# Low value weights in 64 rows: two gates' low products in the two row halves of the array

## The reference, cut to what matters

```python
Pn = rmsnorm(P, input_norm_w)
k_proj, v_proj = Pn @ Wk.T, Pn @ Wv.T
for _ in range(3):
    q_proj = rmsnorm(slots, slot_norm_w) @ Wq.T
    attn = softmax(einsum('bkd,bmd->bkm', q_proj, k_proj) * SCALE, axis=-2)
    attn = attn / (sum(attn, axis=-1) + EPS)
    updates = einsum('bkm,bmd->bkd', attn, v_proj)
    gx, gh = updates @ wih.T + bih, slots @ whh.T + bhh
    r, z = sigmoid(xr + hr), sigmoid(xz + hz)
    n = tanh(xn + r * hn)
    slots = (1.0 - z) * n + z * slots
```

## Time and profile before

| | us |
|---|---|
| median of 3 runs | 1113.85 (1113.64 to 1114.71) |
| the profiled execution | 1113.94 |
| its span in the profile | 1112.2 |
| TensorE busy in the span | 1081.4 (97%) |
| VectorE busy | 779.3 (70%) |
| ScalarE busy | 547.1 (49%) |
| POOL busy | 340.8 (31%) |

### The profile page before, as it was taken

The page is one execution under the profiler, slowest core; times in us unless marked ns, Lnnn a source line. Parts: engine busy times, 40 slices in busy tenths (PEclk is TensorE's granted clock), DMA queues, the critical chain, the costliest instruction groups (busy, mean ns, idle before and its releaser), DMA issues.

```text
span 1112.2 us, 17705 instructions
## 1 busy us (share of the span) xinstructions
PE 1081.4 (97%) x6087; PEld 932.4 (84%) x6087; DVE 779.3 (70%) x1504; ACT 547.1 (49%) x830; POOL 340.8 (31%) x352
## 2 busy tenths in 40 slices
PE   6799999999999999999999999999999999999996
PEld 4588888888887878888888888888889888888896
DVE  7887687868689878888466666566665666656663
ACT  5365555555457843333455544544544554545442
POOL 6124444444206100000214242342333433324332
PEclk9899999999999999999999999999999999999998
DMA  7600110101226541222664543534435444344421
GB/s 246 151 1 16 23 34 6 28 11 24 91 73 193 152 125 23 27 30 27 169 210 103 142 97 132 152 90 137 112 121 148 99 128 135 102 144 116 117 34 20
DMA packets 61323, 105.39 MB, mean 95 GB/s; under 512 B 12128, under 2 KB 50272, under 8 KB 56928
## 3 DMA queue, kind: packets, MB, share of 16 engines
q1 hardware_dynamic: 44064, 83.05, 23.5%
q0 software_dynamic: 16512, 21.50, 12.0%
q10 hardware_dynamic: 704, 0.29, 0.1%
HBM read 74.11 MB, written 21.27 MB: 86 GB/s over the span
## 4 chain that ended last, share of the span: by engine, by line
PE 90%; DVE 6%; ACT 1%; issue 1%; DMA 1%; SPq 0%; POOL 0%; DVEq 0%; ACTq 0%
PE wide L1289 30%; PE down L1303 15%; PE wide L854 15%; PE wide L1142 8%; PE down L1154 4%; PE down L915 3%; PE wide L861 3%; PE wide L863 2%; PE wide L1335 2%; PE side L1275 1%; PE side L1126 1%; PE side L304 1%; PE down L1349 1%; PE side L939 1%; DVE pre L1706 1%
## 5 line engine op out<-in xcount | busy, mean ns | idle before, releaser
L2277 DVE SCALAR_TENSOR_TENSOR hid<-wide,b_up,silu 128x512 f32<-128x512 f32 x120 | 90.1, 751 | 161.5 <-PE wide L1289 152.9
L1289 PE MATMUL wide<-xt_hi,w_hi 128*128 128x512 f32 x480 | 188.6, 393 | 0.0
L1289 PE MATMUL wide<-xt_lo,w_hi 128*128 128x512 f32 x480 | 187.7, 391 | 0.0
L1289 PE MATMUL wide<-xt_hi,w_lo 128*128 128x512 f32 x480 | 186.9, 389 | 0.0
L825 POOL DMA_INDIRECT out_tokens<-y,idx_out x64 | 111.6, 1744 | 222.0 <-DVE y L2258 175.7
L1662 ACT ACTIVATE silu<-wide,b_gate 128x512 f32<-128x512 f32 x120 | 82.1, 684 | 143.7 <-PE wide L1289 143.7
L1303 PE MATMUL down<-w_hi,hid_hi 128*128 128x256 f32 x480 | 136.5, 284 | 0.0
L1303 PE MATMUL down<-w_lo,hid_hi 128*128 128x256 f32 x480 | 135.7, 283 | 0.0
L1303 PE MATMUL down<-w_hi,hid_lo 128*128 128x256 f32 x480 | 135.7, 283 | 0.0
L1671 ACT ACTIVATE hid_hi<-hid 128x512 fp32r<-128x512 f32 x120 | 76.0, 633 | 100.6 <-DVE hid L2277 100.6
L2228 DVE TENSOR_TENSOR w_lo<-raw,w_hi 128x768 fp32r<-128x768 f32 x128 | 121.5, 949 | 2.5 <-ACT w_hi L1636 2.5
(11 more groups left out here) (329 smaller groups left out, 2269.1 us busy)
## 6 DMA issues: line engine op xcount, KB each, us to landing
raw<-in_w_expert SPq DMA_DIRECT2D x32, 1536.0 KB, 6.3
x_raw<-in_x SPq DMA_DIRECT2D x16, 256.0 KB, 6.8
out_tokens<-slots SPq DMA_DIRECT2D x16, 256.0 KB, 3.7
token_rows<-work SPq DMA_DIRECT2D x8, 512.0 KB, 3.0
out_tokens<-y POOLq DMA_DIRECT2D x8, 512.0 KB, 5.9
attn<-rms_c SPq DMA_DIRECT2D x24, 128.0 KB, 2.3
attn<-expo SPq DMA_DIRECT2D x24, 128.0 KB, 2.3
x_first<-in_x SPq DMA_DIRECT2D x8, 256.0 KB, 3.1
```

What stands on the lines that cost most here:

```text
L1289: last = nc.tensor.matmul(bank[:, f % 2, :], w[f // HALF_F][:, f % HALF_F, (c + k) * P:(c + k + 1) * P], x_[:, k, :], start=(m == 1), stop ...
L2277: nc.vector.scalar_tensor_tensor(hid[:, f % 2, :], eup[:, f % 2, :], b_up[:, bass.ds(e, 1), f:f + 1].rearrange("p a b -> p (a b)"), silu[: ...
```

## The change

The tile vw_lo loses one of its two copies: for batch b of a pair, the columns of gates r and x lie in b's own 64 rows and those of gate z in the other 64 rows. The low attention no longer meets the low value weights: vw_lo is multiplied with the high attention alone, in 64 rows. For z that needs the high attention in the other rows too, so each half's high attention is also sent to a new tile attn_x (one for each pair), two more DMAs a half. TensorE closes r and z by `low_gates`: r's low product in b's rows and z's in the other rows, next to each other, behind z's high product. m_r is told there instead of right behind r's products. x's low product (`new_value`) has 64 rows and no partner. POOL subtracts in two instructions, z's 256 columns into vw_f, which SP then moves to the other rows by two DMAs a pair, and r's and x's 512 straight into vw_lo. To make room, the tile dif goes, and the mix works in place in slots.

```diff
-        vw_lo = att("vw_lo", [P, PAIRS, 2, 3 * D], F32R)
+        attn_x0 = att("attn_x0", [P, 2 * GROUP], F32R)
+        att.at += 2 * D * 4
+        vw_lo = att("vw_lo", [P, PAIRS, 3 * D], F32R)
...
-        dif = loop("dif", [P, KC, GROUP])
+        attn_x1 = loop("attn_x1", [P, 2 * GROUP], F32R)
+        attn_x = (attn_x0, attn_x1)
...
-            DMA_ATTN = 2 * 2 * 16
+            DMA_ATTN = 3 * 2 * 16
+            VW_MOVES = (4 + 2) * PAIRS
...
-                    sp.wait_ge(p_own, pair + 1)
-                    move_rows(vw_lo, vw_f, pair)
+                    sp.wait_ge(p_own, 2 * pair + 2)
+                    for b in range(2):
+                        sp.dma_start(vw_lo[rows_of(1 - b), pair, D:2 * D].bitcast(F32), vw_f[rows_of(b), pair, D:2 * D])\
+                            .then_inc(d_vw, 16)
...
                         sp.dma_start(attn[rows_of(b), pair, b, half].bitcast(F32), rms_c[rows_of(b), h, :]).then_inc(d_attn[h], 16)
+                        sp.dma_start(attn_x[pair][rows_of(1 - b), half].bitcast(F32), rms_c[rows_of(b), h, :])\
+                            .then_inc(d_attn[h], 16)
...
-                    nc.gpsimd.tensor_tensor(vw_f[:, pair, :].bitcast(F32R), vw_f[:, pair, :],
-                                            vw_own[:, pair, :].bitcast(F32), ALU.subtract).then_inc(p_own, 1)
+                    nc.gpsimd.tensor_tensor(vw_f[:, pair, D:2 * D].bitcast(F32R), vw_f[:, pair, D:2 * D],
+                                            vw_own[:, pair, D:2 * D].bitcast(F32), ALU.subtract).then_inc(p_own, 1)
+                    nc.gpsimd.tensor_tensor(gates_rx(vw_lo, pair), gates_rx(vw_f, pair), gates_rx(vw_own, pair).bitcast(F32),
+                                            ALU.subtract).then_inc(p_own, 1)
...
-                        nc.tensor.matmul(out[:, :], vw_hi[:, pair, b, cols], attn[:, pair, b, half],
-                                         start=start, stop=False)
-                        return nc.tensor.matmul(out[:, :], vw_lo[:, pair, b, cols], attn[:, pair, b, half],
-                                                start=False, stop=True)
+                        return nc.tensor.matmul(out[:, :], vw_hi[:, pair, b, f * P:(f + 1) * P], attn[:, pair, b, half],
+                                                start=start, stop=False)
+
+                    def low_gates():
+
+                        own, other = rows_of(b), rows_of(1 - b)
+                        nc.tensor.matmul(gate_r[:, :], vw_lo[own, pair, c * P:(c + 1) * P], attn[own, pair, b, half],
+                                         start=False, stop=True).then_inc(m_r, 1)
+                        nc.tensor.matmul(gate_z[:, :], vw_lo[other, pair, (2 + c) * P:(3 + c) * P], attn_x[pair][other, half],
+                                         start=False, stop=True).then_inc(m_z, 1)
+
+                    def new_value():
+
+                        own = rows_of(b)
+                        from_attention(gate_x, 4 + c, True)
+                        nc.tensor.matmul(gate_x[:, :], vw_lo[own, pair, (4 + c) * P:(5 + c) * P], attn[own, pair, b, half],
+                                         start=False, stop=True).then_inc(m_x, 1)
...
                         wait_attention()
-                        from_attention(gate_r, c, False).then_inc(m_r, 1)
-                        from_attention(gate_z, 2 + c, False).then_inc(m_z, 1)
+                        from_attention(gate_r, c, False)
+                        from_attention(gate_z, 2 + c, False)
+                        low_gates()
                     else:
                         if c == 0:
                             wait_attention()
-                        from_attention(gate_r, c, False).then_inc(m_r, 1)
+                        from_attention(gate_r, c, False)
                         if early is not None:
                             early()
                         pe.wait_ge(a_z, u + 1)
                         from_slots(gate_z, 2 + c, False)
-                        from_attention(gate_z, 2 + c, False).then_inc(m_z, 1)
+                        from_attention(gate_z, 2 + c, False)
+                        low_gates()
                         if between is not None:
                             between()
                         pe.wait_ge(a_h, u + 1)
                         from_slots(gate_h, 4 + c, True).then_inc(m_h, 1)
                     pe.wait_ge(v_pre, u + 1)
-                    from_attention(gate_x, 4 + c, True).then_inc(m_x, 1)
+                    new_value()
...
-                    nc.vector.tensor_tensor(dif[:, :, :], slots[:, :, sl], nn[:, :, :], ALU.subtract).then_inc(v_mix, 1)
+                    nc.vector.tensor_tensor(slots[:, :, sl], slots[:, :, sl], nn[:, :, :], ALU.subtract).then_inc(v_mix, 1)
```

More of the change, by code:

```diff
@@ L700, in _, with gates_rx @@
                                         ALU.subtract).then_inc(p_wlo, 1)
+                def gates_rx(tile, pair):
+                    return tile[:, pair, :].rearrange("p (a c) -> p a c", c=D)[:, 0:3:2, :]
                 for pair in range(PAIRS):
                     pool.wait_ge(a_own, pair + 1)
-                    nc.gpsimd.tensor_tensor(vw_f[:, pair, :].bitcast(F32R), vw_f[:, pair, :],
-                                            vw_own[:, pair, :].bitcast(F32), ALU.subtract).then_inc(p_own, 1)
+                    nc.gpsimd.tensor_tensor(vw_f[:, pair, D:2 * D].bitcast(F32R), vw_f[:, pair, D:2 * D],
+                                            vw_own[:, pair, D:2 * D].bitcast(F32), ALU.subtract).then_inc(p_own, 1)
+                    nc.gpsimd.tensor_tensor(gates_rx(vw_lo, pair), gates_rx(vw_f, pair), gates_rx(vw_own, pair).bitcast(F32),
+                                            ALU.subtract).then_inc(p_own, 1)
                 def low_of(g, run):
@@ L858, in from_attention @@
                     def from_attention(out, f, start):
-                        cols = slice(f * P, (f + 1) * P)
-                        nc.tensor.matmul(out[:, :], vw_hi[:, pair, b, cols], attn[:, pair, b, half],
-                                         start=start, stop=False)
-                        return nc.tensor.matmul(out[:, :], vw_lo[:, pair, b, cols], attn[:, pair, b, half],
-                                                start=False, stop=True)
+                        return nc.tensor.matmul(out[:, :], vw_hi[:, pair, b, f * P:(f + 1) * P], attn[:, pair, b, half],
[11 more added lines that the diff above has]
+                                         start=False, stop=True).then_inc(m_x, 1)
                     def wait_attention():
                         if u == 0:
-                            pe.wait_ge(d_vw, PAIRS * 8 * 16)
+                            pe.wait_ge(d_vw, VW_MOVES * 16)
+                            pe.wait_ge(p_own, 2 * PAIRS)
                         pe.wait_ge(d_attn[g4 % 2], DMA_ATTN * (2 * it + pair + 1))
@@ L1713, in gru_group @@
                     dve.wait_ge(a_n, u + 1)
-                    nc.vector.tensor_tensor(dif[:, :, :], slots[:, :, sl], nn[:, :, :], ALU.subtract).then_inc(v_mix, 1)
+                    nc.vector.tensor_tensor(slots[:, :, sl], slots[:, :, sl], nn[:, :, :], ALU.subtract).then_inc(v_mix, 1)
                     dve.wait_ge(v_mix, 2 * g + 1)
                     dve.wait_ge(a_z, u + 2)
-                    nc.vector.scalar_tensor_tensor(dif[:, :, :], tz[:, g4 % 2, :, :], 1.0, dif[:, :, :], ALU.add,
+                    nc.vector.scalar_tensor_tensor(slots[:, :, sl], tz[:, g4 % 2, :, :], 1.0, slots[:, :, sl], ALU.add,
                                                    ALU.mult).then_inc(v_mix, 1)
                     dve.wait_ge(v_mix, 2 * g + 2)
-                    nc.vector.scalar_tensor_tensor(slots[:, :, sl], dif[:, :, :], 0.5, nn[:, :, :], ALU.mult,
+                    nc.vector.scalar_tensor_tensor(slots[:, :, sl], slots[:, :, sl], 0.5, nn[:, :, :], ALU.mult,
                                                    ALU.add).then_inc(v_new, 1)
@@ L2033, in mix_half @@
                     dve.wait_ge(a_n, u + 1)
-                    nc.vector.tensor_tensor(dif[:, c, :], slots[:, c, sl], nn[:, c, :], ALU.subtract).then_inc(v_mix, 1)
+                    nc.vector.tensor_tensor(slots[:, c, sl], slots[:, c, sl], nn[:, c, :], ALU.subtract).then_inc(v_mix, 1)
                     dve.wait_ge(v_mix, m + 1)
                     dve.wait_ge(a_z, u + 2)
-                    nc.vector.scalar_tensor_tensor(dif[:, c, :], tz[:, (GPP - 1) % 2, c, :], 1.0, dif[:, c, :], ALU.add,
+                    nc.vector.scalar_tensor_tensor(slots[:, c, sl], tz[:, (GPP - 1) % 2, c, :], 1.0, slots[:, c, sl], ALU.add,
                                                    ALU.mult).then_inc(v_mix, 1)
                     dve.wait_ge(v_mix, m + 2)
-                    nc.vector.scalar_tensor_tensor(slots[:, c, sl], dif[:, c, :], 0.5, nn[:, c, :], ALU.mult,
+                    nc.vector.scalar_tensor_tensor(slots[:, c, sl], slots[:, c, sl], 0.5, nn[:, c, :], ALU.mult,
```

## The result

The changed kernel takes 1140.99 us (median of 5 runs, 1140.79 to 1149.69) against 1114.43 of the kernel before; the ratio is 1.0261, 95% interval 1.024 to 1.0282. The medians alone give 1.0238; the ratio lies by that of the means, 1.0259, which the slowest of the five pulls up. By the medians it is slower by 26.6 us, where 9.5 were forecast. The profiled execution is the slowest of the five, 1149.69; what sets it apart from the others comes further down.

What follows compares the result with a forecast made beforehand. TensorE, busy for 97% of the span, was taken as the bound; -9.5 + 1.4 + 2.0 + 15.1 + 0.5 = +9.5 on 1113.94 gave 1123.4 us. The range was 1105 to 1145 (forecast case 1114 to 1132, chance 0.38).

Steps and rivals of the forecast that it cites:

- (f): Recurrent part: 192 borders between 128-row and 64-row matmuls, 0.09 us each; +15.1 in 42 units, +0.5 in six.
- The bound of 0.35: Upper price of one border in us: the old stream runs dry, 0.16, then the new weights load, 0.19.
- (b): Six units opening a half iteration: r closes one slot later, so each loses 0.23 us instead of gaining; +1.4.
- The rule on the border: Skill page: switching the tiling mode drains TensorE; with the 0.16 us tail as drain, 1135.6 us, chance 0.12.
- the full drain: Rival: at each border the next stream waits out the last one's 0.16 us tail; +21.7, 1135.6 us, chance 0.12.
- Drain and load: Rival: at each border weights load only behind the drain, 0.35 us; +57.8, 1171.7 us, chance 0.07.
- (a): r's and z's low products stream side by side, saving one 0.227 us slot in each of 42 units; -9.5.
- No overlap: Rival: the pair's two halves stream one behind the other, borders free; +3.4, 1117.3 us, chance 0.10.
- (c): Units other than the opening ones: r's later close hides under h and x products; taken 0, bound 1.5 us.
- (d): More attention DMAs on SP's queue delay the first two attentions by 1.2 and 0.8 us; +2.0.
- (e): Setup: POOL's value-weight subtraction in two instructions, SP's moves down from eight to six per pair; taken 0.

Runs made afterwards that it cites:

- x_full: The changed kernel, but x's low product in all 128 rows, so one stay in 64 rows a unit instead of two: 1126.36 us (1.0114).
- same_half: The changed kernel, but z's low product in the same 64 rows as r's, so the two cannot run side by side: 1156.67 us (1.0387).
- full_early_moves: The changed kernel, but all low products in 128 rows and in the order of the kernel before, extra attention transfers kept: 1115.89 us (1.0015).
- full_early: As full_early_moves without the extra transfers; only the single copy of low value weights and the mix in place remain: 1113.72 us (0.9995).
- double_pair: The changed kernel with the pair of r's and z's low products issued twice in the same stay in 64 rows: 1152.24 us (1.0341).

## Why the prediction was wrong

*(f), the borders,* is the step that failed, by its size. The count (192) and the sign were right. The price was taken as 0.09, "the value of the only row in which the stream is broken at all"; it is 0.20. That row shows one of two parts, the load that nothing hides (0.10 measured). The other, the 0.09 before the load starts, was only in the upper bound, as 0.16. The bound of 0.35 was right in its form (dry, then load) and wrong in both numbers, since it took logged durations, a matmul's tail of 0.16 and a load's 0.19; the starts show 0.09 and 0.10. With 0.20 the same sum gives 42 x (0.80 - 0.227) = 24.1, six opening units at 1.88 - 1.45 = 0.43, 2.6, and 2.0 for the transfers: 28.7, or 1142.6. The runs gave 1140.99; the 1.7 between them is not explained.

The opening unit of the changed kernel, the counterpart of the earlier trace rows: 1.88 from 180.09 to 181.97. Its next unit waits for tr, so what counts is when r closes: 0.23 for the later close of (b) and 0.20 for the one border ahead of it. The other three borders lie under the round trip, as (f) had it (x_full, with two of them gone, still takes 1.88). Of the six units only the price was wrong, 0.20 for 0.09.

```profile
180.09 0.61 PE L874 MATMUL wide<-attn,vw_hi 128*128 128x512 f32 x2
180.63 0.50 PE L880 MATMUL wide<-attn,vw_lo 64*128 64x512 f32 x1
...
181.97 0.50 PE L868 MATMUL wide<-slots_hi,whh_hi 128*128 128x512 f32 x1
```

*The rule on the border* was weighed and given 0.12 of chance and 0.07 with the load. The Trainium skill, TensorEngine Tiling (Array Packing), Key Properties, says that switching the tiling mode drains TensorE. The trace agrees, if the 0.09 is this drain. The rows show a second part beside it: the load ahead stops at the border as well, which costs as much again. The nearest rival to the result, the full drain (1135.6), had the right mechanism by half, and came near because its 0.16 happens to lie close to the sum of both parts, 0.20. Drain and load (1171.7) had both parts and priced each too high.

*(a)* was right: the pair overlaps, 0.00 to 0.01 between its starts. "No overlap" is refuted by these starts and by same_half, which is a slot a unit longer. The Trainium skill, TensorE: Matmul & The Clock Gate, Part 3, gives about 4 ns for a further tile of a pack; the trace agrees within its 0.01.

*(b)* was right in the trace, 1.67 measured for 1.68, without borders; in the times it could not be told.

*(c)* held: ScalarE's later tr and tz add no wait for TensorE; the only waits for them are those of the opening units, 1.4 us in five places against 1.8.

*(d)* was right in size, 2.0 for 2.2 measured (full_early_moves against full_early). The queue of the changed kernel, beside the earlier trace rows:

```profile
46.12 0.46 SPq L563 DMA_DIRECT2D attn<-rms_c  x1
...
48.55 1.24 SPq L568 DMA_DIRECT2D attn<-expo  x2
```

Line 568 begins 2.43 behind the first issue, where line 560 began 1.14 behind: 1.3 later. The first product starts at 51.65 and not at 50.6, as the first issue itself came at 46.12 instead of 45.17. In full_early_moves, with the same transfers and a first issue at 45.04, the two are at 47.47 and 50.56, as forecast; the first issue differs by up to 1.1 us between the profiles, and that the change moves it is not shown.

*(e)* was right: full_early stands at 0.9995. POOL's two instructions take 0.73 and 1.30 us for the 1.85 of the earlier trace rows, under cover.

```profile
29.63 0.73 POOL L715 TENSOR_TENSOR vw_f<-vw_f,vw_own 128x256 fp32r<-128x256 f32 x1 [2.23 <-ACT vw_own L1511]
30.32 1.30 POOL L717 TENSOR_TENSOR vw_lo<-vw_f,vw_own 128x512 fp32r<-128x512 f32 x1
```

## What to carry to other kernels

Packing two 64-row matmuls side by side saves a slot (0.227 us for 512 columns), but a stay in 64 rows among 128-row matmuls costs 0.40, near two slots. By these numbers I estimate that two packed pairs a stay come out about even (0.45 saved for 0.40, before any transfer that the packing needs) and that three gain (0.68 for 0.40); double_pair has two in a stay, but the second only repeats the first, so no run here shows such a gain. So first ask how many such products can stand together; a lone 64-row product, like x's here, only loses. Where half the rows are enough but cannot be paired, fill them up or take all rows: 96 and 128 rows cost the same and break nothing.

## What the runs showed of the hardware beside that

A border between 128 and 64 rows stops the pulling ahead of weights in both directions: the load starts 0.32 behind the matmul before it on the way in, and 0.42 on the way out, where that matmul itself had 0.10 of bare load (288.92 to 289.34). Inside a stay, and between 96 and 128 rows, the next load starts no later than 0.10 behind the matmul before.

TensorE's granted clock falls from 2.4 to 1.2 GHz now and then inside a stream that is nearly full. In the changed kernel one fall follows the sixteen two-column matmuls of the column sums (1.95 us), another a wait of 2.2 us for VectorE's slots. The first kind is in the profile of each of the five kernels that have 64-row stays, once each, and in none of the six that have none, though all run these column sums; why, no run shows. The second kind isn't tied to the borders: full_early_moves, which has none, shows one behind a wait for slots of 1.9 us, which the kernel before also has (2.0) without a fall in its profile. The stretch in full_early_moves:

```profile
350.00:360.00 10.00, 8.06 (x37) 6.74 (x36) 9.76 (x25) 7.39 (x13) 8.64 (x12) 0.83 0.61 190
```

One such fall is some 1.7 us by the estimate above, 0.15% of this kernel, and so sets how small a difference its medians can tell. What decides whether it comes stays open.
